# One edge layer of a graph network: mean, beta and split shift of the second stage, rows squared, and the place of the last group in the scan

## The reference

```python
h = jnp.maximum(_layernorm(x, axis=-1), 0.0)
z = jnp.concatenate([h[source], h[target], edge_attrs], axis=-1)
msg = jax.nn.sigmoid(z @ W_f + b_f) * jax.nn.softplus(z @ W_s + b_s)
message = jax.ops.segment_sum(msg, source, num_segments=N_NODES)
mean = jnp.mean(message, axis=0)
var = jnp.mean((message - mean) ** 2, axis=0)
normed = (message - mean) * jax.lax.rsqrt(var + BN_EPS) * gamma + beta
return x + h + normed
```

## Time and profile before

| | us |
|---|---|
| median of 3 runs | 1060.56 (1060.47 to 1061.27) |
| profiled execution | 1060.81 |
| its span | 1059.1 |

### The profile page before, as it was taken

How to read it: one execution, slowest core, us unless ns; L and a number is a source line. 1 busy time by engine, 2 the same in 40 slices (tenths; PEclk the granted TensorE clock), 3 DMA queues, 4 the chain that set the end, 5 groups by cost and what they waited for, 6 DMA issues and landing times.

```text
span 1059.1 us, 11028 instructions
## 1 busy us (share of the span) xinstructions
PE 631.5 (60%) x2458; PEld 453.8 (43%) x2458; DVE 733.2 (69%) x1547; ACT 540.0 (51%) x1181; POOL 729.9 (69%) x652
## 2 busy tenths in 40 slices
PE   0474665666566666656766666676556689944232
PEld 0252444454444444444544454554445578810000
DVE  3884675757575686766777666776666569699788
ACT  1263654545454665545565464655646564434322
POOL 6777878787877877777878777787878752430700
PEclk9855565555555565556555555655656689955555
DMA  8997534343434334333443333433433399799999
GB/s 320 397 394 275 126 96 106 96 106 94 106 94 106 74 86 87 61 81 61 79 87 61 80 71 70 87 63 79 85 56 59 35 380 420 247 302 426 413 404 377
DMA packets 88183, 176.07 MB, mean 166 GB/s; under 512 B 42575, under 2 KB 49299, under 8 KB 79699
## 3 DMA queue, kind: packets, MB, share of 16 engines
q1 hardware_dynamic: 35851, 115.32, 30.9%
q0 software_dynamic: 42880, 20.09, 15.4%
q10 hardware_dynamic: 9416, 40.29, 9.3%
HBM read 107.12 MB, written 68.53 MB: 166 GB/s over the span
## 4 chain that ended last, share of the span: by engine, by line
POOL 48%; DMA 24%; issue 17%; DVE 6%; PE 3%; ACT 1%; SPq 1%; POOLq 0%; ACTq 0%; DVEq 0%
POOL msgs_dram L607 24%; POOL m_buf L594 24%; DMA m_buf<-msgs_dram 8%; DMA msgs_dram<-y_kept 8%; DMA msgs_dram<-sums,target 6%; PE ps_all L1544 2%; DVE m_buf L1795 2%; DMA out_dram<-m_buf 2%; DVE m_buf L1801 1%; DVE sums L1717 1%; PE ps_all L1539 0%; SPq L499 0%; POOL m_buf L617 0%; DVE target L794 0%; DVE m_buf L763 0%
## 5 line engine op out<-in xcount | busy, mean ns | idle before, releaser
L594 POOL DMA_INDIRECT m_buf<-in_x_dram,m_buf x384 | 366.9, 955 | 118.7 <-issue 109.4
L607 POOL DMA_INDIRECT msgs_dram<-sums,target x184 | 289.7, 1574 | 56.2 <-issue 55.8
L1171 PE MATMUL ps_all<-sums,m_last 128*128 128x64 f32 x920 | 188.5, 394 | 124.8 <-ACT m_last L1033 107.1
L1171 PEld LDWEIGHTS ps_all<-sums,m_last 128*128 128x128 f32 x920 | 181.0, 303 | 136.2 <-issue 112.5
L719 DVE TENSOR_REDUCE m_last<-late 128x24 f32<-128x1536 f32 (+1 forms) x49 | 85.3, 1742 | 87.8 <-ACT late L984 87.8
L1131 PE MATMUL ps_all<-ident,m_buf 128*128 128x128 f32 x192 | 53.0, 431 | 128.6 <-DVE m_buf L809 128.6
L1145 PEld LDWEIGHTS ps_all<-m_buf 128*128 128x128 f32 x392 | 91.9, 322 | 49.0 <-issue 49.0
L794 DVE TENSOR_TENSOR target<-moved,m_last 128x4 int32<-128x4 f32 x49 | 9.6, 196 | 146.1 <-POOLq L605 145.8
L1033 ACT ACTIVATE m_last<-m_last,one_col 128x512 f32<-128x512 f32 x196 | 107.6, 550 | 1.6
L1131 PEld LDWEIGHTS ps_all<-ident,m_buf 128*128 128x128 f32 x192 | 34.9, 217 | 160.4 <-DVE m_buf L809 138.5
L1143 PE MATMUL ps_all<-m_buf 128*128 128x512 f32 x98 | 98.8, 1111 | 0.0
(11 more groups left out here) (171 smaller groups left out, 1078.1 us busy)
## 6 DMA issues: line engine op xcount, KB each, us to landing
m_buf<-msgs_dram SPq DMA_DIRECT2D x38, 1024.0 KB, 11.9
m_buf<-in_x_dram SPq DMA_DIRECT2D x48, 512.0 KB, 5.0
msgs_dram<-y_kept SPq DMA_DIRECT2D x14, 1536.0 KB, 11.0
out_dram<-m_buf ACTq DMA_DIRECT2D x20, 1024.0 KB, 11.2
m_buf<-src_rows_dram SPq DMA_DIRECT2D x47, 256.0 KB, 4.1
y_spill_dram<-y_kept ACTq DMA_DIRECT2D x19, 512.0 KB
y_kept<-y_spill_dram SPq DMA_DIRECT2D x8, 1024.0 KB, 12.1
m_buf<-in_x_dram,m_buf POOLq DMA_INDIRECT x392, 2.5
```

What stands on the lines that cost most here:

```text
L594: pool.indirect_dma_start(xg[:, n % G_SLOTS, 2 * j + c, :], None, x, bass.IndirectOffsetOnAxis(ap=ids[:, c, n * TILES + j:n * TILES + j + ...
L607: pool.indirect_dma_start(msgs, bass.IndirectOffsetOnAxis(ap=target[:, n % UNROLL, j:j + 1], axis=0), comb[:, n % COMB_SLOTS, j, :], None, ...
L1171: pe.matmul(ps_c[:, j, :], same_of(b, j, j + 1)[:, 0, :], msg_of(g)[:, b, :], start=(b == 0 and not begun), stop=(b == j), skip_group_chec ...
```

## The change

- The first group of blocks with 18 rows squared is 1 to 9 instead of 4 to 12; behind it, and in block 0, 20 rows of 32 are squared, also in blocks 22 and 23. Three banks are used from block 17 on instead of 19.
- The six steps of the last group at blocks 0 to 2 of ScalarE's and VectorE's lists (centring to rstd and normalising, and copy_before) stand ahead of the scan; all other steps move three blocks forward, `FINISH_AT` from 13 to 10, `CORRECT_AT` from 15 to 12. TensorE waits for `comb_copied` ahead of `turn_edges`.
- `take_mean` is gone, and the beta rows. All parts get the split shift from TensorE, so shift and `split_shift` stand ahead of the first multiplication, and the first four parts, still copied in the scan, get their row behind the split.

```diff
--- before.py
+++ after.py
@@ -78,23 +78,20 @@
 FREE_FIRST = 3
 SQ_ROWS = 20
 SQ_BESIDE = 18
-BESIDE = range(4, 13)
-SQ_THEN_ROWS = 16
+BESIDE = range(1, 10)
+SQ_THEN_ROWS = 20
 SQ_FIRST = (6, 2)
 SQ_THEN = (6, 4, 5)
-SQ_CHANGE = 19
+SQ_CHANGE = 17
 Y_ROWS = 32
 BANK_ROWS = 8
 PSUM_BANKS = 8
 Y_FIRST = 4
 Y_BLOCK = 19
 Y_AHEAD = 4
-FINISH_AT = 13
-CORRECT_AT = 15
+FINISH_AT = 10
+CORRECT_AT = 12
 WHOLE = 1.5 * 2.0 ** 23
-BETA_PARTS = Y_FIRST + 2
-FEW_SQUARED = 2
-FEW_ROWS = 12
 LAST_PIECES = ((0, 16, 8), (16, 8, 0), (24, 5, 5))
 SPLIT = 3
 
@@ -1196,6 +1193,7 @@
                 ins = pe.transpose(ps_z[:, j, :], xc_last[:, 2 * j:2 * j + 2, :].rearrange("p c f -> p (c f)"),
                                    ident[:, :])
             ins.then_inc(z_turned, 1)
+            pe.wait_ge(comb_copied, PRE)
             turn_edges(g_last)
 
         def join_last(t):
@@ -1271,7 +1269,6 @@
     shift_ready = sem("shift_ready")
     split_steps = sem("split_steps")
     split_done = sem("split_done")
-    mean_taken = sem("mean_taken")
     scale_ready = sem("scale_ready")
     scaled = sem("scaled")
     y_copied = sem("y_copied")
@@ -1307,8 +1304,6 @@
         n = BLOCKS[b][1]
         if b == NB - 1:
             return list(LAST_PIECES)
-        if b >= NB - 1 - FEW_SQUARED:
-            return [(0, n, FEW_ROWS)]
         return [(0, n, n * (SQ_ROWS if b < BESIDE.start else SQ_BESIDE if b in BESIDE else SQ_THEN_ROWS) // S_BLK)]
 
     def wait_piece(eng, b, j):
@@ -1467,6 +1462,9 @@
                 act.wait_ge(y_loaded[order[i]], 16 * len(y_pieces(order[i])))
             act.activation(ps_y(k), y_of(order[i])[:, r:r + n, :], ACT.Copy).then_inc(y_copied, 1)
 
+        last.square()
+        last.rstd()
+        last.copy_before()
         act.wait_ge(banks_blank, 1)
         for k, (b, r, n, j) in enumerate(chunks):
             if added_before(k):
@@ -1477,20 +1475,14 @@
             act.activation(ps_sq(k)[:, 0:n, :], m_scan(b, r, n), ACT.Square).then_inc(rows_squared, 1)
             if r == BANK_ROWS:
                 if b == 0:
-                    last.copy_before()
+                    last.less_source()
                 elif b == 1:
-                    last.square()
+                    last.copy_turned()
                 elif b == 2:
-                    last.rstd()
+                    last.mark_same()
                 elif b == 3:
-                    last.less_source()
+                    last.softplus_log()
                 elif b == 4:
-                    last.copy_turned()
-                elif b == 5:
-                    last.mark_same()
-                elif b == 6:
-                    last.softplus_log()
-                elif b == 7:
                     last.gates()
                 elif b == FINISH_AT:
                     last.copy_comb()
@@ -1530,13 +1522,14 @@
         def clear(bank):
             return clear_bank(pe, at, bank)
 
-        def add_row(k, weights, row):
+        def add_row(k):
 
             _, _, n = y_parts[k]
             pe.wait_ge(y_copied, k + 1)
             for c in range(0, n, BANK_ROWS):
                 w = min(BANK_ROWS, n - c)
-                ins = pe.matmul(ps_y(k)[:, c:c + w, :], weights, row.unsqueeze(1).to_broadcast([row.shape[0], w, F]),
+                ins = pe.matmul(ps_y(k)[:, c:c + w, :], ones_b[:, :],
+                                shift_row[0:SPLIT, :].unsqueeze(1).to_broadcast([SPLIT, w, F]),
                                 start=False, stop=True, skip_group_check=True)
             ins.then_inc(y_summed, 1)
 
@@ -1553,15 +1546,15 @@
                     ins = cross(m_scan(b, r, w).rearrange("p r f -> p (r f)"), w * F, not begun)
                     begun = True
             ins.then_inc(block_crossed, 1)
-            if b == 3:
+            if b == 0:
                 last.turn()
-            elif b == 4:
+            elif b == 1:
                 last.products()
-            elif b == 5:
+            elif b == 2:
                 last.join(0)
-            elif 7 <= b < 12:
-                last.join(b - 6)
-            elif b == 12:
+            elif 4 <= b < 9:
+                last.join(b - 3)
+            elif b == 9:
                 last.join(6)
                 last.join(7)
                 last.combine()
@@ -1571,9 +1564,6 @@
                 for bank in sorted(set(range(PSUM_BANKS - 1)) - set(SQ_FIRST)):
                     ins = clear(bank)
                 ins.then_inc(banks_blank, 1)
-            if Y_BLOCK < b <= Y_BLOCK + Y_FIRST:
-                pe.wait_ge(affine_loaded, 32)
-                add_row(b - Y_BLOCK - 1, ones[0:1, :], bet[0:1, :])
             if b == M_BUFS:
                 pe.wait_ge(rest_loaded, 16)
                 cross(m_rest[:, :], F, False)
@@ -1589,11 +1579,9 @@
         pe.matmul(ps_tot, ones[:, :], sq_tail[:, :], start=False, stop=True).then_inc(total_ready, 1)
         pe.wait_ge(var_ready, 1)
         clear(PSUM_BANKS - 1).then_inc(banks_blank, 1)
-        for k in range(Y_FIRST, BETA_PARTS):
-            add_row(k, ones[0:1, :], bet[0:1, :])
         pe.wait_ge(split_done, 1)
-        for k in range(BETA_PARTS, len(y_parts)):
-            add_row(k, ones_b[:, :], shift_row[0:SPLIT, :])
+        for k in range(len(y_parts)):
+            add_row(k)
 
     def gpsimd(pool):
 
@@ -1694,21 +1682,15 @@
             dve.wait_ge(chain, 1)
             dve.tensor_tensor(mean2[:, :], mean[:, :], mean[:, :], ALU.mult).then_inc(chain, 1)
 
-        def take_mean(k):
-
-            i, r, n = y_parts[k]
-            m = m_out(i, r, n)
-            dve.wait_ge(rows_squared, chunks_of(order[i]))
-            dve.wait_ge(block_crossed, order[i] + 1)
-            dve.tensor_tensor(m, m, mean[:, :].unsqueeze(1).to_broadcast([P, n, F]), ALU.subtract
-                              ).then_inc(mean_taken, 1)
-
         def correct():
 
             dve.wait_ge(corr_steps, 4)
             dve.tensor_reduce(corr_row[:, :], was_read.rearrange("p t f -> p f t"), AX.X, ALU.add
                               ).then_inc(corr_done, 1)
 
+        last.centre()
+        last.sum_squares()
+        last.normalise()
         last_piece = len(chunks) - 1
         for k, (b, _, n, _) in enumerate(chunks[:last_piece]):
             dve.wait_ge(rows_squared, k + 1)
@@ -1718,23 +1700,17 @@
                               ALU.add).then_inc(rows_added, 1)
             if k + 1 < chunks_of(b):
                 continue
-            if b == 0:
-                last.centre()
-            elif b == 1:
-                last.sum_squares()
-            elif b == 2:
-                last.normalise()
-            elif b == 4:
+            if b == 1:
                 last.mask(0)
-            elif b == 6:
+            elif b == 3:
                 last.mask(1)
                 last.softplus()
-            elif b == 7:
+            elif b == 4:
                 last.message()
                 last.mask(2)
-            elif 8 <= b < 11:
-                last.mask(b - 5)
-            elif b == 11:
+            elif 5 <= b < 8:
+                last.mask(b - 2)
+            elif b == 8:
                 last.mask(6)
                 last.mask(7)
             elif b == FINISH_AT:
@@ -1742,8 +1718,6 @@
                 take_means()
             elif b == CORRECT_AT:
                 correct()
-            if order[0] + 2 <= b < order[0] + 2 + BETA_PARTS:
-                take_mean(b - order[0] - 2)
         dve.wait_ge(rows_added, last_piece)
         dve.tensor_reduce(sq_row[:, :], sq_acc[:, :, :].rearrange("p r f -> p f r"), AX.X,
                           ALU.add).then_inc(acc_reduced, 1)
@@ -1765,7 +1739,8 @@
         dve.tensor_tensor(scale[:, :], var[:, :], gam[:, :], ALU.mult).then_inc(scale_ready, 1)
         dve.wait_ge(scale_ready, 1)
         dve.tensor_tensor(mean2[:, :], mean[:, :], scale[:, :], ALU.mult).then_inc(chain, 1)
-        dve.wait_ge(mean_taken, BETA_PARTS)
+        dve.wait_ge(chain, 3)
+        dve.tensor_tensor(shift[:, :], bet[:, :], mean2[:, :], ALU.subtract).then_inc(shift_ready, 1)
 
         def split_shift():
 
@@ -1787,15 +1762,13 @@
                 if k < SPLIT - 1:
                     dve.wait_ge(split_steps, 2 * SPLIT + k)
 
+        split_shift()
         for k, (i, r, n) in enumerate(y_parts):
-            if k == BETA_PARTS:
-                split_shift()
             m = m_out(i, r, n)
             wait_m(dve, i)
+            if i < len(held):
+                dve.wait_ge(block_crossed, order[i] + 1)
             dve.tensor_tensor(m, m, scale[:, :].unsqueeze(1).to_broadcast([P, n, F]), ALU.mult).then_inc(scaled, 1)
-            if k == 0:
-                dve.wait_ge(chain, 3)
-                dve.tensor_tensor(shift[:, :], bet[:, :], mean2[:, :], ALU.subtract).then_inc(shift_ready, 1)
             dve.wait_ge(scaled, k + 1)
             dve.wait_ge(y_summed, k + 1)
             dve.tensor_tensor(m, m, ps_y(k), ALU.add).then_inc(added, 1)
```

## The result

The changed kernel takes 1064.0 us (median of eight runs, 1063.02 to 1064.76), the kernel before 1060.51 in the same comparison (eight runs, 1060.09 to 1061.86): the ratio is 1.0031, with a 95% interval of 1.0023 to 1.004. It is slower, by more than the 0.2% that can be told from no change. 1062.0 had been forecast; the time lies in the wide range (1057.5 to 1066) and outside the forecast's own narrower one (1059.5 to 1062.7), close to what the rival "the ring of scan buffers starves DMA" gives (1064.5). The profiled execution took 1064.07 us with a span of 1062.3; that of before took 1060.81 with 1059.1, so the two traces differ by 3.3 us.

What follows compares the result with a forecast made beforehand. A chain between two DMA-paced stretches was taken as the bound, VectorE replacing TensorE. First stores come 1.8 us later, of which 1.2 reaches the end: 1060.81 + 1.2 = 1062.0 us; own range 1059.5 to 1062.7, wide range 1057.5 to 1066.

Steps and rivals of the forecast that it cites:

- the ring of scan buffers starves DMA: Slower rival: late sum_kept delays block 11's crossing, so block 18's load; 1064.5 us, chance 0.28 shared with longer VectorE stretch.
- The bound: Two stretches run at DMA's pace; a chain from last crossings to first store holds the 25 us between.
- TensorE no longer the bound: Late scan: 26 fewer crossings (6.7 us) and four beta rows (4.2 us) let TensorE end 10 us earlier; VectorE bounds.
- VectorE's times: Last group to stage two: adds resume 891.4, VectorE ends 921.0, 3.5 us later; first add 929.4, 1.8 later.
- the 0.6 for a late square on ScalarE: Blocks 11 to 16: with two banks, ScalarE's square ends after the short third add; 0.6 us (0 to 1.4).
- The lower clock from diagonal to variance: After its wait TensorE runs ten records between diagonal and variance at 1.2 GHz: 1.1 us more (0 to 1.1).
- This gate stays: Reload of messages behind the twelve late adds stays at 943, since they start from the scan's landing at 914.4.
- The gate a fixed time behind the landing: Late adds start from the landing, not the variance; last add 935.63, SyncE through at 943.27, as before.
- The faster rival (VectorE isn't held): finish() slips past GpSimd's additions (888.6) and TensorE's clock stays up: chain 3.9 us shorter, 1058.1 us, chance 0.22.
- The moved steps at nothing: Centring, squares and normalising moved ahead of the scan, under the first load's wait: cost nothing; 3 us without that cover.

Runs made afterwards that it cites:

- The split done alone: Kernel before with mean and beta work out of the scan and the split shift for all parts, rows and last group unmoved: 1059.24 us (0.9989).
- letting GpSimd wait: Changed kernel with GpSimd's additions waiting for sum_kept and the correction one block later: 1061.73 us (ratio 1.0016 to the kernel before).
- the clears later: Changed kernel with TensorE's wait for sum_kept and its clears behind block 13 instead of 10: 1062.04 us (ratio 1.0014 to the kernel before).
- the copy later: Changed kernel with ScalarE issuing copy_comb behind the third chunk of block FINISH_AT: 1062.17 us (ratio 1.0015 to the kernel before).
- the three kernels that have the move and not the chunk: The move alone, 1058.76 us; split and move, 1058.68; split and move with TensorE's sum_kept wait and clears at block 13 instead of 10, 1058.41.
- The move alone: Kernel before with only the last group begun three blocks earlier (BESIDE 1 to 9, FINISH_AT 10, CORRECT_AT 12): 1058.76 us (0.9984).
- split and move: Changed kernel with 16 rows squared behind BESIDE (1 to 9), 12 in blocks 22 and 23, three banks from block 19: 1058.68 us (0.9982).
- the third alone: Kernel before with only 20 rows squared and 12 crossed from block 13 on, third bank still at block 19: 1066.52 us (1.0055).
- the two kernels that differ in it: Split and move (0.9982), and the same with BESIDE at blocks 4 to 12, so block 10 keeps three chunks: 1062.97 us (1.0027).
- both waits mended: Changed kernel with sum_kept wait and clears at block 13 and copy_comb behind block FINISH_AT's third chunk: 1060.87 us (ratio 1.0003 to the kernel before).

## Why the prediction was right or wrong

**The bound: right.** Two stretches at the pace of DMA, and a gap that a chain holds. The account above is that reading in bytes. In bytes it is also better than in shares: 890 to 962 has a share of 0.89 before and after, at 313 and 301 GB/s.

**TensorE no longer the bound: right.** No wait at the diagonal in the changed kernel. The split done alone, which takes the mean work and four beta rows out of the scan, brings the diagonal 5 us forward. The count of crossings is right (26 fewer), the place not quite: 29 fewer behind block 9, three more ahead of it.

**VectorE's times: right to about half a microsecond.** Last joins 879.6 forecast, 880.12 measured; ScalarE's copy 884.3 and 884.94; finish() from 885.4 and 885.97, held by both additions; adds resumed 891.4 and 891.81; reduction 921.0 and 921.27; first addition of stage two 929.4 and 928.87. Some 0.6 of each is the later start of this execution's scan. The terms for VectorE's end add up to 921.3, not to the 921.0 that was written down. From 891.81 to 921.27 the blocks took what was worked out (28.1 us), the correction 1.4 instead of 1.2, and the 0.6 for a late square on ScalarE did not come: no wait for ScalarE stands there. finish() has twelve small operations, eleven of which were not held before, where the prediction counted nine of eleven. That the small operations are held was shown by letting GpSimd wait: 0.15 and 0.16 us. The Trainium skill's rule (SBUF — State Buffer, Who interferes with whom), by which the one that comes second waits for the whole instruction, agrees with every run here for operations with two inputs in SBUF. Of the two held operations on which the prediction rested it, the one for the mean has a single input, so only the other bears out the rule as the prediction put it.

**The lower clock from diagonal to variance: not in this run.** 1.1 us was counted; 1.84 us lay between the two, as before, at a granted clock of 1.00 (2.4 GHz; window of 922). With the clears later the clock was 0.50 in that window and the wait for TensorE 2.23 instead of 1.16 us, so the term exists, in some kernels and not in others; it lay in my bounds (0 and 1.1). It went the other way with the clears: there 1.25 us was counted for the rival and 2.31 came, behind a wait of 5.17 us for sum_kept, with the clock at 0.50 (1.2 GHz).

**"This gate stays": wrong, the step that failed.** The forecast moved the first stores by 1.8 us and held the reload at 943, because the late adds start from the landing. So they do, and the landing didn't stay: 919.41 instead of 914.43, 953.13 instead of 943.27. The reason is the one told in the rival. sum_kept came at about 891.4, the clears ended at 893.7, block 11 was crossed at the lower clock, and block 18 was asked for at 896.70 (894.7 in the rival). The rival's own price was the right size: + 3.7 on the profiled run against + 3.3 measured. Its chance of 0.28 was too low, seen from here, for a case whose steps stood in the prediction's own numbers: block 18 asked for at 894.7, block 17 landed at 894.8. There was no slack between two times that each carry half a microsecond of error. Block 18 was asked for 2.0 later than that, and each error (0.5 on sum_kept, 1.06 on the clears, 0.4 on the crossing behind them) went the bad way. That the time still lies in the wide range is no merit of the forecast's sum, which had this gap at nothing; it is the rival's mechanism that was measured.

**The gate a fixed time behind the landing: wrong too.** Before they took 21.2 us from first to last and the reload came 7.6 after the last was issued. After, with the landing 5 us later, the last is issued at 942.23, 22.8 after the first, and the reload follows 10.9 later. A landing 5 us late became a gate 9.9 us late. That the adds run into the first stores is a guess that fits; no run tested it. In the account this doesn't cost 9.9 us, since stores and y loads move bytes meanwhile, at a lower rate; how much of the 0.86 MB it is apart from the ring's gap isn't settled: with the copy later the reload stayed at 951.85 and 0.4 of the 0.86 MB were back, with the clears later it was at 945.34 and all of them were.

**The faster rival (VectorE isn't held)** didn't come about with the change as it stands. The prediction had put the hold down to the third chunk, and that holds: the three kernels that have the move and not the chunk show all small operations of finish() but the last unheld, and all three are faster than before.

**The moved steps at nothing: nearly.** The move alone gains 1.7 us, so what it moves is covered; but it has the dip at 884 to 890 in all kernels with the move, 0.3 to 0.5 MB, 0.7 to 1.3 us, which I had at zero. Which buffer is late there, and whether it comes of the first stages or of the later steps, wasn't tested.

**What stays open**: why split and move don't add up. With both, the bytes say 3.7 us and the median 1.9, the profiled execution being that kernel's fastest. The chain then waits on loads and the reload at 944 is where it was; a run with the late adds started earlier would tell, and wasn't made.

## What to carry to other kernels

Take each part of a change by its own worth before the sum: here two parts gain 1.2 and 1.7 us and the third alone costs 5.8. Most of that cost is one more chunk ahead of one wait (4.8 us between the two kernels that differ in it); with both waits mended, 2.1 us are left for the longer chain of adds. Where a buffer ring feeds DMA, write down for each buffer when it is asked for and when the load ahead of it lands; where the two are within the error of the estimate, the gap belongs into the forecast. And count bytes up to the last stretch that runs at full rate: it gave the differences of eleven kernels from before to 0.6 us, where busy shares gave 0.9 for 3.3.

## What the runs showed of the hardware

- A GpSimd addition of 1.80 us held the VectorE operations on SBUF alone that fell on it to its end, also small ones: 0.16 us became 1.32 to 1.76, and 0.26 for the mean's square became 1.79. VectorE's adds, which take one of their two inputs from PSUM, were not held: seven of them took 4.96 us from 891.20 beside the addition of 891.28 in the kernel where GpSimd waits, about what seven adds take at 0.79 and 0.52 us from one to the next without it (4.9). The operation for the mean, whose only tensor is msg_sum, was held too (886.79, 1.54 us in split and move, to the end of the addition at 888.28; as before), where the Trainium skill (SBUF — State Buffer, Who interferes with whom) speaks of two SBUF inputs, and of tensor_scalar in its two-port modes. In which mode it ran no trace here shows.
- The issue of a late add took 1.54 to 1.75 us in most cases, but single ones beside the first stores took up to 3.15 (935.11 in the split alone, 938.78 in the changed kernel; one such in eight of the twelve traces). With the clears later none took over 1.75, though its adds went on to 937.28. What sets it off isn't known.
- A DMA share close to 1 isn't full rate: 0.94 at 304 GB/s in 930 to 962 of the changed kernel, 1.04 at 413 behind it. The window of the changed kernel:

```profile
930.00:962.00 32.00, 13.05 (x29) 2.79 (x26) 31.66 (x21) 11.95 (x7) 11.95 (x7) 0.50 0.94 304
```
